# Two parts of a graph network kernel changed together: the self loop's term, and the last stage's accumulators and loop

## What is computed

```python
# graph part, two layers (loops: every node is also its own neighbour)
h = layer_norm(x)                     # first relu and norm in front, not shown
xw = h @ W
out = segment_sum(dinv[row] * dinv[col] * xw[row], col)   # row, col: edges and self loops
h = relu(out + b + h @ lw.T + lb)
x_final = h0 + h1;  x1 = x + x_final @ pw.T + pb
# tensor-product part on x1: per edge, weights from an MLP on 8 edge features
x0, x1 = up-projection of relu(norm(x1))          # 128 + 128*3
m0, m1 = products of the weights, the sender's row and edge_attr_4
msg = segment_sum(m, receiver);  out = x1 + (msg @ W_out) / 10
```

## Time and profile before

| what | value |
|---|---|
| median of 3 runs | 5402.21 us (5398.03 to 5405.94) |
| profiled execution | 5398.43 us |
| its span (first to last instruction) | 5396.6 us |
| TensorE busy / VectorE / ScalarE / GpSimd | 88% / 52% / 41% / 50% |
| TensorE's granted clock, mean | 0.941 of full |
| indirect gathers in the two layers (L547) | 1584 |
| edge matmuls in the two layers (L1289) | 3904 |
| segment-sum matmul instructions in the last stage (L1415) | 3520 |
| pairs in the last stage (L1123, one for each) | 440 |

### The profile page before, as it was taken

How to read it: one execution, slowest core, us unless ns; L and a number is a source line. 1 busy time by engine, 2 the same in 40 slices (tenths; PEclk the granted TensorE clock), 3 DMA queues, 4 the chain that set the end, 5 groups by cost and what they waited for, 6 DMA issues and landing times.

```text
span 5396.6 us, 99589 instructions
## 1 busy us (share of the span) xinstructions
PE 4750.2 (88%) x15182; PEld 2032.8 (38%) x15183; DVE 2801.5 (52%) x6919; ACT 2239.5 (41%) x6181; POOL 2719.5 (50%) x3416
## 2 busy tenths in 40 slices
PE   7899887778889888677788789999999999999999
PEld 5344222223344323233344433333333344444443
DVE  7543012233445201223344467777777777777776
ACT  0443222111223222111222366666666666666665
POOL 0332666666666466676666444444444444334332
PEclk9999898888999898788898999999999999999999
DMA  2232776667778677777788744444444444444443
GB/s 84 92 109 96 213 215 201 212 215 234 236 237 260 188 216 216 214 223 246 247 259 265 225 126 126 124 122 128 124 129 128 125 125 126 128 125 125 129 127 107
DMA packets 434963, 921.11 MB, mean 171 GB/s; under 512 B 63349, under 2 KB 171125, under 8 KB 434790
## 3 DMA queue, kind: packets, MB, share of 16 engines
q0 software_dynamic: 197120, 646.08, 40.8%
q1 hardware_dynamic: 182918, 245.65, 13.4%
q10 hardware_dynamic: 54880, 28.91, 1.8%
HBM read 791.98 MB, written 128.41 MB: 171 GB/s over the span
## 4 chain that ended last, share of the span: by engine, by line
PE 62%; issue 12%; DVE 8%; another core or an unknown queue 7%; DVEq 5%; DMA 3%; ACT 1%; ACTq 1%; POOL 0%; SPq 0%; POOLq 0%
PE bank L1415 21%; PE bank L1289 12%; PE bank L1405 6%; PE bank L1244 3%; PE bank L1246 3%; PE bank L1334 3%; PE bank L1336 2%; DVE dense_w L1140 2%; DMA ef<-in_ef_t_dram 2%; PE bank L1268 1%; PE bank L1350 1%; DVE hA L1131 1%; PE bank L1438 1%; PE bank L1280 1%
## 5 line engine op out<-in xcount | busy, mean ns | idle before, releaser
L547 POOL DMA_INDIRECT ring<-tab_d,idx x1584 | 1566.1, 989 | 785.8 <-issue 471.8
L1289 PE MATMUL bank<-ring,ohp 128*128 x3904 | 1073.8, 423 | 348.5 <-issue 259.6
L796 ACT ACTIVATE dense_w<-hA,hC 128x128 f32<-128x128 f32 x2640 | 819.3, 389 | 703.7 <-DVE hA L1127 519.7
L514 POOL DMA_INDIRECT ring<-up_d,idx x880 | 855.2, 972 | 501.8 <-POOL idx L510 352.4
L1415 PE MATMUL bank<-dense_w,yb 128*128 128x512 f32 x1760 | 934.6, 613 | 1.5 <-DVE dense_w L1144 1.5
L1415 PE MATMUL bank<-dense_w,oh 128*128 128x512 f32 x1760 | 898.7, 592 | 0.0
L1289 PEld LDWEIGHTS bank<-ring,ohp 128*128 x3904 | 401.8, 104 | 997.5 <-issue 706.0
L1035 DVE TENSOR_TENSOR ohp<-iota_w,dst_f 128x512 f32 x392 | 268.2, 693 | 761.1 <-remote 259.6
L510 POOL COPY idx<-src_i 128x2 int32 x440 | 80.8, 184 | 860.8 <-DVE dense_w L1144 813.8
L1405 PE MATMUL bank<-w,hC 64*128 64x512 f32 x1760 | 498.3, 643 | 11.6 <-DMA hC<-hid_d 11.6
L1415 PEld LDWEIGHTS bank<-dense_w,oh 128*128 128x128 f32 x1760 | 334.4, 190 | 420.9 <-issue 420.9
(11 more groups left out here) (190 smaller groups left out, 5308.1 us busy)
## 6 DMA issues: line engine op xcount, KB each, us to landing
hC<-hid_d SPq DMA_DIRECT2D x440, 64.0 KB
ring<-tab_d,idx POOLq DMA_INDIRECT x1584
tab_d<-tout SPq DMA_DIRECT2D x98, 256.0 KB, 2.7
tw<-tab_d SPq DMA_DIRECT2D x98, 256.0 KB
hlw<-hl_d SPq DMA_DIRECT2D x98, 256.0 KB
hid_d<-hC ACTq DMA_DIRECT2D x98, 256.0 KB
hl_d<-agg SPq DMA_DIRECT2D x74, 256.0 KB, 3.0
ring<-up_d,idx POOLq DMA_INDIRECT x880
```

The source lines that it names most:

```text
L514: g_.indirect_dma_start(ring_v[:, b, k, :], None, table, bass.IndirectOffsetOnAxis(idx_t[:, b, k:k + 1], 0)).then_inc(S["got"][b], 16)
L547: g_.indirect_dma_start(ring_h[:, slot, k, :], None, table, bass.IndirectOffsetOnAxis(idx_b[:, slot, k:k + 1], 0)).then_inc(S["got"][slot] ...
L796: ac.mul(msg[:, b, k, 1, P + m * P:2 * P + m * P], t2[:, b, k, :], yg[:, b, 4 * k + 1 + m:4 * k + 2 + m])
L1289: ins = pe.matmul(bank[0][:, :], ohp_b[:, bass.ds(at, 1), k, :].rearrange("p b n -> p (b n)"), ring_b[:, bass.ds(slot, 1), k, h, :].rearra ...
```

## The change

Five things are done at once.

- The self loop's term is no longer a pair of matmuls in each window. `dsq` = dinv² is computed once; where the linear term `hl_out` (dense stage) or `agg` (layer 1's `low`) is made, VectorE adds dsq times the product's bank to it with one more operation after a drain. The load of `tw`, its semaphores and the two matmuls go. `layer_out` now waits for the last visit (`used`). The linear term's first operation and its wait for the old store stand ahead of the table's low half.
- In the last stage windows take banks 0, 1 and banks 6, 7 by turns (`sums`). A window's first matmul in a bank clears it, `touch` goes, and turning and output product use the old window's own banks.
- `keep_a`, `keep_b` and the turn come after the next window's first two pairs, `copy_mT` and `out_product` after its fourth, `finish` after its last.
- All of this needs at least four pairs ahead of a loop, and the last window two after it, so MINV becomes 7. The same ranges serve the two layers.
- The per-pair code of VectorE and ScalarE is written out twice and not four times: the ring slot is addressed by a register. GpSimd waits for each pair's rows and tells both by one semaphore (`arrived`).

```diff
@@ -31,7 +31,7 @@
...
-MINV = 4
+MINV = 7
...
@@ -303,16 +302,24 @@
...
+        def over_sets(eng, window):
+
+            window(0, 0)
+            with eng.Fori(0, NW // 2 - 1) as j:
+                window(j * 2 + 1, 1)
+                window(j * 2 + 2, 0)
+            window(NW - 2, 1)
+            window(NW - 1, 0)
...
@@ -327,9 +334,15 @@
...
-        m_bank = [bank[6], bank[7]]
+
+        def sums(w, h):
+
+            if isinstance(w, int):
+                return ps[:, 6 * (w % 2) + h, :]
+            return ps[:, bass.ds(w % 2 * 6 + h, 1), :].rearrange("p b n -> p (b n)")
+
...
@@ -390,10 +403,6 @@
...
-                def load_self(w, S=S, L=L):
-                    after(sp, S["sum_done"], w)
-                    sp.dma_start(tw[:, :], rows(tab_d[L], w)).then_inc(S["self_in"], 16)
...
@@ -504,6 +513,7 @@
...
+                        landed = g_.snap((n + (buffers - 1 - LAG)) // buffers * 32)
...
@@ -513,8 +523,15 @@
...
+                            with g_.If(n > LAG):
+                                g_.wait_ge(S["got"][(b - LAG) % buffers], landed)
+                                g_.nop().then_inc(S["arrived"], 1)
...
@@ -978,10 +998,13 @@
 
             def table_low(tile, q, b):
                 ve.wait_ge(n_hi, tile + 1)
+                after(ve, hl_st[b], q, 16)
+                ve.tensor_tensor(hl_out[b][:, :], bank[4 + b][:, :], bia["b0"][:, :], ALU.add)
                 ve.scalar_tensor_tensor(out=tout[:, b, D:], in0=bank[2 + b][:, :], scalar=col(dup[:, 0, :], tile),
                                         in1=tout[:, b, 0:D], op0=ALU.mult, op1=ALU.subtract).then_inc(n_out, 1)
-                after(ve, hl_st[b], q, 16)
-                ve.tensor_tensor(hl_out[b][:, :], bank[4 + b][:, :], bia["b0"][:, :], ALU.add).then_inc(n_hl, 1)
+                ve.drain()
+                ve.scalar_tensor_tensor(out=hl_out[b][:, :], in0=bank[2 + b][:, :], scalar=col(dsq, tile),
+                                        in1=hl_out[b][:, :], op0=ALU.mult, op1=ALU.add).then_inc(n_hl, 1)
...
@@ -1052,8 +1075,8 @@
...
-                def layer_out(w, S=S, L=L):
-                    ve.wait_ge(S["sum_done"], w + 1)
+                def layer_out(w, S=S, L=L, c=c):
+                    ve.wait_ge(S["used"], ve.snap(c) + (NV - 1))
...
@@ -1072,10 +1095,13 @@
...
+                    after(ve, S["hl_stored"], w, 16)
+                    ve.tensor_tensor(agg[:, :], bank[3][:, :], bia["b1"][:, :], ALU.add)
                     ve.scalar_tensor_tensor(out=tout[:, 0, D:], in0=bank[2][:, :], scalar=col(dup[:, 1, :], w),
                                             in1=tout[:, 0, 0:D], op0=ALU.mult, op1=ALU.subtract).then_inc(S["tab_ready"], 1)
-                    after(ve, S["hl_stored"], w, 16)
-                    ve.tensor_tensor(agg[:, :], bank[3][:, :], bia["b1"][:, :], ALU.add).then_inc(S["hl_ready"], 1)
+                    ve.drain()
+                    ve.scalar_tensor_tensor(out=agg[:, :], in0=bank[2][:, :], scalar=col(dsq, w), in1=agg[:, :],
+                                            op0=ALU.mult, op1=ALU.add).then_inc(S["hl_ready"], 1)
...
@@ -1116,13 +1142,14 @@
...
-                def pair(ub):
-                    b, u = ub % 2, ring_u[:, ub, :, :]
+                u = ring_u[:, bass.ds(ve.snap(n % NU), 1), :, :].rearrange("p b k n -> p (b k) n")
+
+                def pair(b):
...
-                    ve.wait_ge(M["got"][ub], ve.snap((n + (NU - 1)) // NU * 32))
+                    ve.wait_ge(M["arrived"], n)
...
@@ -1143,59 +1170,61 @@
...
+            def keep_b(w, behind=0):
+                ve.wait_ge(M["seg_done"], ve.snap(c) + (1 - behind))
+                after(ve, M["turned"], w)
+                ve.tensor_copy(mB[:, :], sums(w, 1)).then_inc(M["mB"], 1)
...
+            def window(w):
+
+                lo, hi = ve.snap(lo_r), ve.snap(hi_r)
+                if not isinstance(w, int) or w > 0:
+                    with ve.Fori(lo, lo + 2) as g:
+                        messages(g)
+                    keep_b(w - 1, 2)
+                    with ve.Fori(lo + 2, lo + 4) as g:
+                        messages(g)
+                    copy_mT(w - 1)
+                    lo = ve.snap(lo + 4)
+                if not isinstance(w, int) or w < NW - 1:
+                    next_range(w + 1)
+                with ve.Fori(lo, hi) as g:
                     messages(g)
...
                 if not isinstance(w, int) or w > 0:
                     finish(w - 1)
...
+                ve.drain()
+
...
@@ -1314,10 +1343,6 @@
...
-                    pe.wait_ge(S["self_in"], (w + 1) * 16)
-                    pe.matmul(bank[0][:, :], ident_h[:, :], tw[:, 0:D], start=False, stop=False, skip_group_check=True)
-                    pe.matmul(bank[0][:, :], ident_h[:, :], tw[:, D:], start=False, stop=True,
-                              skip_group_check=True).then_inc(S["sum_done"], 1)
...
@@ -1406,78 +1431,72 @@
...
-                        ins = pe.matmul(bank[h][:, :], (oh0, oh)[h][:, b, k, :], msg[:, b, k, h, :], start=False,
-                                        stop=(last and k == 1), skip_group_check=True)
+                        ins = pe.matmul(sums(p, h), (oh0, oh)[h][:, b, k, :], msg[:, b, k, h, :], start=(first and k == 0),
+                                        stop=False, skip_group_check=True)
...
-                after(pe, M["mT_a"], w)
-                after(pe, M["mT_b"], w)
-                after(pe, M["out_ready"], w)
...
-                    ins = pe.transpose(m_bank[i // 4][:, (i % 4) * P:(i % 4 + 1) * P], sr, ident[:, :])
+                    ins = pe.transpose(sums(p, i // 4)[:, (i % 4) * P:(i % 4 + 1) * P], sr, ident[:, :])
...
-            def window(w):
+            def window(w, p):
                 lo, hi = window_range(pe, w)
-                after(pe, M["mA"], w)
-                after(pe, M["mB"], w)
-                touch(bank[0][:, :], D, True)
-                touch(bank[1][:, :], D, True)
+                if not isinstance(w, int) or w > 1:
+                    pe.wait_ge(M["out_ready"], w - 1)
+                step(p, first=True)
+                step(p)
                 if not isinstance(w, int) or w > 0:
-                    turn_m(w - 1)
-                step(True)
+                    turn_m(w - 1, 1 - p)
+                with pe.Fori(lo + 2, lo + 4) as g:
+                    step(p)
+                if not isinstance(w, int) or w > 0:
+                    out_product(w - 1, 1 - p)
                 if not isinstance(w, int) or w < NW - 1:
-                    step(True)
-                    if not isinstance(w, int) or w > 0:
-                        out_product(w - 1)
-                    with pe.Fori(lo + 2, hi - 1) as g:
-                        step(True)
-                    step(True, True)
+                    with pe.Fori(lo + 4, hi) as g:
+                        step(p)
...
+                    with pe.Fori(lo + 4, hi - 2) as g:
+                        step(p)
+                    step(p, ahead=False)
+                    step(p, ahead=False)
...
```

More of the change, by code:

```diff
@@ L807, in first_pair @@
                 ac.reg_mov(hi_r, hi)
-                weigh(lo)
-            def second_pair(w):
-                weigh(ac.snap(lo_r) + 1)
-            def rest(w):
-                with ac.Fori(ac.snap(lo_r) + 2, ac.snap(hi_r)) as g:
-                    weigh(g)
-            def keep_a(w):
-                more = 1 if isinstance(w, int) and w == NW - 1 else 0
-                ac.wait_ge(M["seg_done"], ac.snap(c) + more)
-                after(ac, M["turned"], w)
-                ac.copy(mA[:, :], bank[0][:, :]).then_inc(M["mA"], 1)
@@ L838, in _, with keep_a, copy_mT @@
-            first_pair(0)
+            def keep_a(w, behind=0):
+                ac.wait_ge(M["seg_done"], ac.snap(c) + (1 - behind))
+                after(ac, M["turned"], w)
+                ac.copy(mA[:, :], sums(w, 0)).then_inc(M["mA"], 1)
+            def copy_mT(w):
+                times = ac.snap(turned_r)
+                after(ac, M["o_done"], w)
+                ac.wait_ge(M["turned"], times)
+                ac.reg_add(turned_r, turned_r, 1)
+                ac.copy(mT[:, 0:4, :], sums(w, 0).rearrange("p (c n) -> p c n", c=4)).then_inc(M["mT_a"], 1)
```

122 lines of the change are left out of this document (55 added, 67 removed).

## The result

The changed kernel takes **5901.9 us** (median of 4 runs, 5894.8 to 5905.2) against 5404.1 us on the same chip (4 runs). The ratio is 1.0917, with a 95% interval of 1.0896 to 1.0939. The forecast was 5825 us and the prediction's text gives a range of 5700 to 5900. So the sign and the main cost held, the size was 77 us short (2 us beyond that range), and the wait that the change was to take out of the last stage stayed. The profiled execution's span went from 5396.6 to 5900.4 us, by 503.8 us.

The account below looks back on a forecast made before the run. Gathers were taken to set the pace in the two layers, TensorE to bound the dense and last stages. From the profiled 5398.4 us, +381 +155 -69 -42 +2 gave 5825 us, range 5700 to 5900.

Parts of the forecast that it names:

- 66 blocks in the layers: Two layers: MINV 7 lengthens 23 late windows, adding 33 blocks a layer at 5.77 us each, +381 us.
- self loop: Windows: two matmuls of 0.22 us and waits for tw go from each; between 0 and -85 us, taken as -42.
- surplus gathers behind layer 2: Gathers behind the end, 15 us, were said to run beside the working off of layer 1's tail; no cost.
- 33 pairs in the last stage: Last stage: 33 more pairs of TensorE work at 4.71 us each, +155 us.
- turnover: Last stage's window ends: 48 waits of 1.0 us and 49 clearings of 0.43 us go, no new wait, -69 us.
- the two bounds, 186 and 430: Layers' added blocks: +186 us at 5.09 us a block without late windows' own cost, +430 at 6.51 us.
- the gathers are hidden: Rival, 8%: GpSimd's idle time pays for new gathers; a layer block costs only TensorE's 1.77 us visit, 117 us; 5561 us.
- not slower: Rival, 2%: idle time in late layer windows holds all 33 added blocks a layer, full self-loop gain; 5399 us.
- sign of being wrong: Late windows under 5.1 or over 6.5 us a block, or segment sums waiting for VectorE or ScalarE at window starts.
- the turnover keeps a wait: Rival, 10%: in the last stage TensorE's 1.0 us wait a window stays in another place, +48 us; 5873 us.
- The register-addressed operations of VectorE: Last stage: eight a pair cost nothing, being set up while the operation before runs.
- the clock falls: Rival, 4%: TensorE's clock sits at 1.2 GHz, half speed, in late layer windows, +299 us; 6124 us.

Follow-up runs that it names:

- minv7: The kernel before with MINV changed from 4 to 7 and nothing else: 5986.2 us, ratio 1.0981.
- The second group: Runs on one chip where the kernel before took 5213.4 us; the changed kernel once more took 5640.4 us, ratio 1.0825, and with MINV = 5 5152.2 us.
- early: The changed kernel with `finish` moved ahead of a window's last pair on VectorE: 5923.8 us, ratio 1.0871.

## Why the prediction was right, and where it was off

The profiled executions differ by 503 us where the sum had 427. Term by term, from the traces before and after:

| term | forecast | measured |
|---|---|---|
| 66 blocks in the layers | +381 | +366 to +391 |
| self loop | -42 | -9 to -34 |
| (these two together) | (+339) | (+357) |
| waits for agg in layer 1's tail | +2 | about 0 |
| surplus gathers behind layer 2 | 0 | +8 |
| 33 pairs in the last stage | +155 | +155 |
| turnover | -69 | -17 |
| sum | +427 | +503 |

Ahead of the last stage the change lost 365 us (3129.4 to 3494.7). 8 of them are behind layer 2, so 357 are the blocks' and the self loop's together; the trace doesn't part them, and the self loop's 9 to 34 us above give the blocks 366 to 391. The last stage lost 138.3, less 33 x 4.70 = 155 that is -17.

- **The blocks: right.** That is 5.55 to 5.92 us a block against 5.77 forecast. minv7, without the self loop's part, lost 376 us ahead of the last stage within its own group, 5.6 us a block with the 8 us behind layer 2 taken off. Reading the price from window pairs of the trace before, with the window's own cost separated from the block's, is what held; the two bounds, 186 and 430, were far apart, and the choice to keep 5.77 rather than 5.09 was right for this chip. The second group's 5.0 shows that it is not a constant of the kernel, and that the choice had some luck in it. The rival "the gathers are hidden" (1.77 us a block) and "not slower" fell: 1.77 would have been 117 us.
- **The pairs: right**, 4.70 us against 4.71; minv7's last stage alone says +156.
- **The turnover: wrong, the largest error.** The step that failed is "What TensorE may then wait is 0 to 0.5 us a window, 0 to 24 us; I take 0". The prediction's own sign of being wrong, segment sums that wait for VectorE at each window's start, is what the trace shows. The rival that stood beside it at 10%, "the turnover keeps a wait", named the price: 48 us, and 44.4 us were found. So here the rival came true and the forecast did not, and even its 5873 us is 29 short. The prediction set VectorE's 1.41 us of iota and `finish` against 1.26 us of air and 1.16 us of lead, and took the load of the range for the cause of the late one-hot. That load has moved and the one-hot comes no sooner: 2.5 us behind the last messages (5155.52 to 5158.05), where the earlier trace rows had 2.3; the median of the 48 ends, taken from the start of the last operation, went from 2.68 to 2.97 us. From these messages to the next ones VectorE needs 6.35 us (5155.52 to 5161.87). TensorE took up the first of them 0.90 us later, at 5156.42, and would be back after a pair, 4.69 us: 5.59 us in all, 0.8 less than VectorE needs. In the experiment early, where `finish` stands ahead of the last pair, the waits fall to 10.0 us and an end to 2.8 us, near the forecast's 2.5.
- **The self loop: too large.** The step that was off is "I take -42 us, since it is the window cost of 1.7 us that it comes out of". Two matmuls of 0.22 us left the engine that waits for gathers in most windows. The first two stretches of the two layers, 44 windows in all, differ from the earlier trace rows by -5, -5, -1 and +5 us, -6 together, where 44 of the 98 windows were to bring 19. That the same edit could lengthen the last stage by 24 to 27 us, as it did alone, was in no term; in the change it did not show.
- **Behind layer 2: a term that was set at nothing.** The surplus gathers were said to run "beside the 33 us in which layer 1's tail is worked off", and in layer 1 they do (239.8 us between its output 48 and layer 2's first, 238.4 after). Behind layer 2 they run beside the stores of x that the last stage waits for, and that part grew by 8 us.
- **The register-addressed operations of VectorE: right as to TensorE.** They show as 79.9 us of "issue" in front of L1163, 0.17 us a pair, where 34.8 us of idle time stood in front of the same operation before; the air of a pair holds it. At the window's end it is part of the 6.35 us above.
- **The two places of the Trainium skill.** Read as a rate, the fit in the Trainium skill's page "DMA: Bandwidth & Descriptors" (Anatomy of one DMA) makes a block 10.4 us by the prediction's estimate; the runs measured 5.0 to 5.9. In the lengthened windows the granted clock fell from 0.97 to 0.90 in layer 1, where TensorE's busy share went from 93% to 78%, and from 0.93 to 0.86 in layer 2, which agrees with what the prediction cites from the Trainium skill's page "TensorE: Matmul & The Clock Gate" (The HAM clock gate). It stayed far from the half speed of the rival "the clock falls".

The errors are 52 us in the turnover, 18 in blocks and self loop together and 8 behind layer 2, less 2: 76. That the time came out only 2 us beyond 5900 is so because the range had room for a dearer block and a smaller self loop; the turnover's share of it was 24 us, and the turnover was off by 52.

## What to carry to other kernels

A size that sets the shape of a loop (here the least number of pairs in a window) is paid in every stage that shares it; count what it adds before weighing what the loop saves, and give each stage its own where only one needs it. When a wait is taken out of one engine's window end, add up everything that the next engine does between its last and its first pair, its "issue" time too, and set that sum against its lead, not each piece against a pair's idle time. And an edit in one stage can lengthen another: read every stage of the profile after, also those that the edit doesn't touch.

## What the runs showed of the hardware that was not expected

- Chips differ in the stages that gathers pace, and only there: the same 53 blocks took 318 us on one chip and 285 on another, while the change's last stage took 2405.6 and 2404.0, and the first gather of all fourteen traces started between 532 and 536 us. The kernel before spread from 5213 to 5454 us over the groups, 4.6%, and the value of one and the same version went from 80 to 33 us with it.
- VectorE's sequencer cost is not the same for the same loop: 122.6 us of "issue" in front of the one-hot became 291.6 with not one line of the stage edited, and the stage 24 and 27 us longer, in two runs on two chips. The shortest step over the loop's end was 1.17 us in these two and 1.07 in three runs of the loop as it was. The cause is open.
- Twenty gathers of 256 KB that nobody reads, in place of eight, went with a longer wait for the stores beside them: at most 9.3 to 16.2 us in five traces, 5.7 to 6.7 in nine.
